# Second-pass masks moved to GpSimd fills, and a new order on four engines, in an attention and expert kernel

## The reference, cut to what matters

```python
xn = layernorm(x)                                   # x: (2, 1024, 256)
# causal attention, 16 heads of 16, with a linear position bias
scores = einsum(q, k) * 16**-0.5 + (pos_k - pos_q) * slope[h]
scores = where(pos_k > pos_q, -inf, scores)
attn = maximum(softmax(scores), 1e-10)
s = (attn @ v) @ out_w.T + out_b
# feed-forward: RMS norm, router over 32 experts, top 4, at most 128 rows each
y[e] = (silu(rows[e] @ w_gate[e]) * (rows[e] @ w_up[e])) @ w_down[e]
g = silu(xn + sum_of_chosen(w * y) + sigmoid(x @ w_sg) * shared_ffn(x))
out = x + s * g
```

## Time and profile before

| | |
|---|---|
| time, median of 3 runs | 646.54 us (644.6 to 648.15) |
| profiled execution, its own time | 642.44 us |
| span of the profiled execution | 640.8 us |
| TensorE busy | 562.8 us, 88% |
| VectorE busy | 475.2 us, 74% |
| ScalarE busy | 452.6 us, 71% |
| GpSimd busy | 269.1 us, 42% |
| mean granted clock of TensorE | 0.957 of 2.4 GHz |

### The profile page before, as it was taken

The page is one execution under the profiler, slowest core; times in us unless marked ns, Lnnn a source line. Parts: engine busy times, 40 slices in busy tenths (PEclk is TensorE's granted clock), DMA queues, the critical chain, the costliest instruction groups (busy, mean ns, idle before and its releaser), DMA issues.

```text
span 640.8 us, 17285 instructions
## 1 busy us (share of the span) xinstructions
PE 562.8 (88%) x4584; PEld 384.2 (60%) x4584; DVE 475.2 (74%) x1066; ACT 452.6 (71%) x1053; POOL 269.1 (42%) x632
## 2 busy tenths in 40 slices
PE   1699559688999899999999999999999999999992
PEld 1694227555666566666666666666666666666661
DVE  5997964657777867886787788777867886787465
ACT  2322564358877878887888788878888887888670
POOL 7630000215445355445544554455455345544403
PEclk9759869789999999999999999999999999999997
DMA  8991256552335334433444343434433436731147
GB/s 258 167 253 59 99 155 195 132 135 60 88 90 111 91 86 87 105 90 89 102 100 97 91 103 84 92 83 102 98 90 87 105 91 199 192 77 23 26 137 135
DMA packets 79537, 71.47 MB, mean 112 GB/s; under 512 B 18114, under 2 KB 70020, under 8 KB 79492
## 3 DMA queue, kind: packets, MB, share of 16 engines
q1 hardware_dynamic: 70292, 59.30, 34.1%
q0 software_dynamic: 9136, 11.80, 12.1%
q10 hardware_dynamic: 80, 0.03, 0.0%
HBM read 47.82 MB, written 23.59 MB: 111 GB/s over the span
## 4 chain that ended last, share of the span: by engine, by line
PE 49%; ACT 20%; issue 12%; DVE 10%; DMA 4%; SPq 3%; ACTq 1%; DVEq 0%; POOLq 0%; POOL 0%
ACT PSB L1062 10%; PE PSB L897 7%; PE PSB L791 6%; ACT PB L1071 6%; PE PSB L765 5%; PE PSB L813 5%; PE PSB L868 4%; PE PSB L810 4%; PE PSB L787 3%; PE PSB L889 3%; PE PSB L850 2%; PE PSB L666 2%; PE PSB L761 2%; DVE WDS L1281 2%; SPq L497 1%
## 5 line engine op out<-in xcount | busy, mean ns | idle before, releaser
L1346 DVE TENSOR_REDUCE NEGM<-PSB 128x1 f32<-128x1024 f32 (+7 forms) x256 | 192.2, 751 | 58.6 <-PE PSB L765 57.6
L1062 ACT ACTIVATE PSB<-PSB,NEGM 128x1024 f32<-128x1024 f32 (+7 forms) x256 | 183.5, 717 | 35.6 <-DVE NEGM L1346 35.4
L1071 ACT ACTIVATE PB<-PSB 128x128 f32<-128x128 f32 (+7 forms) x256 | 166.8, 653 | 35.5 <-PE PSB L791 33.6
L1352 DVE TENSOR_SCALAR PB<-PB 128x128 f32<-128x128 f32 (+7 forms) x256 | 114.2, 455 | 45.9 <-ACT PB L1071 44.4
L765 PE MATMUL PSB<-STACKS 111*128 111x512 bf16 (+3 forms) x384 | 105.8, 330 | 0.0
L791 PE MATMUL PSB<-STACKS 111*128 111x512 bf16 (+3 forms) x384 | 104.2, 326 | 0.0
L787 PE MATMUL PSB<-MK,IDB 128*128 128x128 bf16 x256 | 57.5, 225 | 22.7 <-ACT PSB L1062 16.4
L1656 POOL DMA_INDIRECT moe_rows<-YE,IDX x32 | 56.9, 1777 | 29.3 <-issue 29.3
L810 PE MATMUL PSB<-PB,VH 128*32 128x256 f32 x640 | 67.8, 384 | 0.0
L787 PEld LDWEIGHTS PSB<-MK,IDB 128*128 128x128 bf16 x256 | 24.5, 96 | 63.7 <-ACT PB L1071 39.2
L761 PE MATMUL PSB<-MQ,IDB 128*128 128x128 bf16 x256 | 58.2, 227 | 0.9 <-ACT UL L1049 0.5
(11 more groups left out here) (200 smaller groups left out, 1171.6 us busy)
## 6 DMA issues: line engine op xcount, KB each, us to landing
STACKS<-q_parts SPq DMA_DIRECT2D x192, 32.0 KB, 1.9
STACKS<-k_parts SPq DMA_DIRECT2D x192, 32.0 KB, 1.8
WGU<-in_L_ffn_w_gate_dram SPq DMA_DIRECT2D x32, 176.0 KB
WGU<-in_L_ffn_w_up_dram SPq DMA_DIRECT2D x32, 176.0 KB
WDS<-in_L_ffn_w_down_dram SPq DMA_DIRECT2D x32, 176.0 KB
q_parts<-PB SPq DMA_DIRECT2D x8, 384.0 KB, 2.6
XN<-in_L_attn_qkv_dram SPq DMA_DIRECT2D x4, 512.0 KB, 5.7
moe_rows<-XN SPq DMA_DIRECT2D x1, 2048.0 KB, 8.8
```

The source lines that it names most:

```text
L1062: act.activation(sc, sc, ACT.Exp, bias=NEGM[:, par, i:i + 1], accum_out=LSUM[:, par, i:i + 1]).then_inc(exp1_done, 1)
L1071: act.activation(PB[:, k % 2, prob_offset(s):prob_offset(s) + (s + 1) * P], psf[:, base:base + (s + 1) * P], ACT.Exp).then_inc(exp2_done, 1)
L1346: dve.tensor_reduce(NEGM[:, par, i:i + 1], psf[:, base:base + (i + 1) * P], AX_X, ALU.max, negate=True).then_inc(max_ready, 1)
L1352: dve.tensor_scalar(p, p, FLOOR, 0.0, ALU.subtract, ALU.max).then_inc(clamp_done, 1)
```

## The change

- `PB` gets another layout, in which the diagonal blocks of tiles 0 to 3, and those of tiles 4 to 6, are evenly spaced, so that one access pattern (`diagonal`) covers each group.
- In the second pass the mask product is left out for seven of the eight tiles; the score product starts the sum itself. In its place GpSimd fills the wrong half of the diagonal blocks in `PB` with 0 after the clamp (`fill_diagonal`): once for tiles 0 to 3 (512 columns, after the clamp of step 3), once for tiles 4 to 6 (384 columns, after the clamp of step 6). The first value batch waits for the second fill instead of the clamp.
- GpSimd's gather stands directly behind the scatter. The first fill comes behind the value copy, the second at the end of the phase.
- VectorE takes the 896-column maximum ahead of the clamp of the unit before (step 7) and of this unit's step 0. It also takes over the copy to `XET`, after its 768-column maximum.
- ScalarE does the weighing behind `exp_seed` and the 896-column exponential instead of ahead of them.
- After the last unit, early products 0 and 1 take the place of gates 4 and 5, and these gates come later.

```diff
@@ -83,9 +83,20 @@
 def prob_offset(s):
-    return s * (s + 1) // 2 * P
+    return 9 * P * s if s < NQ // 2 else P * (10 * (NQ - 1 - s) + 1)
+def diagonal(probs, tiles):
+    n = len(tiles)
+    if tiles.start < NQ // 2:
+        first, step, at = prob_offset(tiles.start), 9 * P, 0
+    else:
+        first, step, at = prob_offset(tiles[-1]) - 9 * P, 10 * P, 9 * P
+    return probs[:, first:first + step * n].rearrange("p (n c) -> p n c", c=step)[:, :, at:at + P]
+FILLED = (range(0, 4), range(4, 7))
 VALUE_BATCH = (range(0, 7), range(7, 8))
 LEAD = 2
 PROJECT_BANK = [2, 6, 7, 2, 6, 7, 2, 3]
@@ -299,6 +310,7 @@
         p2_ready = sem("p2_ready")
         exp2_done = sem("exp2_done")
         clamp_done = sem("clamp_done")
+        fill_done = sem("fill_done")
         pv_done = sem("pv_done")
         v_ready = sem("v_ready")
         o_evacuated = sem("o_evacuated")
@@ -784,12 +796,14 @@
                     pe.wait_ge(exp2_done, unit(it, k, NQ, s - 1))
                 w = P * (NQ - j)
                 key = KS[slot][0:ROWS, j * P:(j + 1) * P]
-                pe.matmul(psf[:, base:base + P], IDB[:, :], MK[:, :],
-                          start=True, stop=False, skip_group_check=True)
+                masked = s == NQ - 1
+                if masked:
+                    pe.matmul(psf[:, base:base + P], IDB[:, :], MK[:, :],
+                              start=True, stop=False, skip_group_check=True)
                 for c0 in reversed(range(0, w, 512)):
                     c1 = min(c0 + 512, w)
                     ins = pe.matmul(psf[:, base + c0:base + c1], key, QS[slot][0:ROWS, j * P + c0:j * P + c1],
-                                    start=(c0 > 0), stop=True, skip_group_check=True)
+                                    start=(c0 > 0 or not masked), stop=True, skip_group_check=True)
                 ins.then_inc(p2_ready, 1)
             def values(it, k, batch):
@@ -800,7 +814,10 @@
                     pe.wait_ge(o_evacuated, unit(it, k))
                     pe.wait_ge(v_ready, unit(it, k, 1, 1))
                     pe.wait_ge(c_turned, unit(it, k, 1, 2) if exists(it, k + 1) else UNITS)
-                pe.wait_ge(clamp_done, unit(it, k, NQ, VALUE_BATCH[batch][-1] + 1))
+                if batch == 0:
+                    pe.wait_ge(fill_done, unit(it, k, len(FILLED), len(FILLED)))
+                else:
+                    pe.wait_ge(clamp_done, unit(it, k, NQ, NQ))
                 for s, c in value_order(batch):
                     j, far = step_tile(s), NQ - 1 - c
                     probs = PB[:, par, prob_offset(s):prob_offset(s) + (s + 1) * P].rearrange("p (t q) -> p t q", q=P)
@@ -1135,10 +1152,6 @@
                 for s in range(NQ):
                     if s == 0 and exists(it, w - 1):
                         shared(it, w - 1, SB)
-                    if s == 2 and exists(it, w):
-                        o = aux_task(it, w, TR)
-                        act.activation(XET[:, :, :].rearrange("p c m -> p (c m)"), o[:, 0:D], ACT.Copy)\
-                            .then_inc(xet_ready, 1)
                     if s == 4 and exists(it, w):
                         shared(it, w, SA)
                     if s == 6 and exists(it, w):
@@ -1147,12 +1160,12 @@
                         exp2(it, k, s, exists(it, k + 2))
                     if s == 0 and isinstance(it, int) and k == UNITS - 2:
                         exp_seed(it, k + 1)
-                    if s == 1 and exists(it, w - 1):
-                        weigh(it, w - 1)
                     if s == 1 and exists(it, k + 1) and not (isinstance(it, int) and k == UNITS - 2):
                         exp_seed(it, k + 1)
                     if exists(it, k + 2):
                         exp1(it, k + 2, s)
+                    if s == 1 and exists(it, w - 1):
+                        weigh(it, w - 1)
                     if isinstance(it, int) and k == UNITS - 2 and s >= NQ - 3:
                         projected(s - (NQ - 3))
                     if isinstance(it, int) and k == UNITS - 1 and s == 0:
@@ -1351,6 +1364,12 @@
                 p = PB[:, k % 2, prob_offset(s):prob_offset(s) + (s + 1) * P]
                 dve.tensor_scalar(p, p, FLOOR, 0.0, ALU.subtract, ALU.max).then_inc(clamp_done, 1)
+            def turn_rows(it, k):
+                b, before = aux(it, k, TR)
+                dve.wait_ge(aux_ready[b], before + 1)
+                dve.tensor_copy(XET[:, :, :].rearrange("p c m -> p (c m)"), PSB[:, AUX + b, 0:D]).then_inc(xet_ready, 1)
             def turn_shift(it, k):
                 dve.wait_ge(c_flipped, unit(it, k, 1, 1))
@@ -1447,16 +1466,22 @@
                 w = k + LEAD
                 for s in range(NQ):
                     if isinstance(it, int) and k == UNITS and s == 1:
-                        for g in (4, 5):
-                            gate(g)
+                        for g in range(2):
+                            early_product(g)
+                    late = exists(it, k + 2) and exists(it, k - 1)
+                    if s == 1 and late:
+                        row_max(it, k + 2, s)
+                        clamp(it, k - 1, NQ - 1)
                     if s > 0 and exists(it, k):
                         clamp(it, k, s - 1)
-                    if exists(it, k + 2):
+                    if exists(it, k + 2) and not (s == 1 and late):
                         row_max(it, k + 2, s)
                     if s == 0 and exists(it, w - 1):
                         shared(it, w - 1, SB)
-                    if s == 0 and exists(it, k - 1):
+                    if s == 0 and exists(it, k - 1) and not late:
                         clamp(it, k - 1, NQ - 1)
+                    if s == 2 and exists(it, w):
+                        turn_rows(it, w)
                     if s == 3 and exists(it, k - 1):
                         evacuate_heads(it, k - 1)
                     if isinstance(it, int) and k == UNITS - 1 and s >= 3:
@@ -1476,10 +1501,10 @@
                         hidden_turned(it, w)
             phases(dve, phase)
-            for g in range(6, NT // 2):
+            for g in range(2, NT // 4):
+                early_product(g)
+            for g in range(NT // 4, NT // 2):
                 gate(g)
-            for g in range(NT // 4):
-                early_product(g)
             for g in range(NT // 4, NT // 2):
                 product(g)
                 add_input(g)
@@ -1542,6 +1567,14 @@
             pool.wait_ge(bias_ready, 1)
             pool.memset(VH[:, :, :, :], 0.0).then_inc(const_ready, 1)
             pool.wait_ge(xn_ready, NT)
+            def fill_diagonal(it, k, part):
+                tiles = FILLED[part]
+                hold(pool, clamp_done, unit(it, k, NQ, tiles[-1] + 1))
+                d = diagonal(PB[:, k % 2, :], tiles)
+                pool.affine_select(out=d, in_=d, compare_op=ALU.is_ge, fill=0.0, base=0,
+                                   pattern=[[0, len(tiles)], [1, P]], channel_multiplier=-1).then_inc(fill_done, 1)
             def chain(it, k):
@@ -1672,10 +1705,12 @@
                     chain(it, k + 1)
                 if exists(it, w - 1):
                     scatter(it, w - 1)
+                if exists(it, w + 1):
+                    gather(it, w + 1)
                 if exists(it, k + 1):
                     prepare_values(it, k + 1)
-                if exists(it, w + 1):
-                    gather(it, w + 1)
+                if exists(it, k):
+                    fill_diagonal(it, k, 0)
                 if exists(it, w) and w % SLOTS == 0:
                     copy_scales(it, w)
                     if w >= SLOTS:
@@ -1685,6 +1720,8 @@
                     b, before = aux(it, w - 1, SB)
                     hold(pool, aux_ready[b], before + 1)
                     copy_block(it, w + 1)
+                if exists(it, k):
+                    fill_diagonal(it, k, 1)
             phases(pool, phase, 1)
```

## The result

The changed kernel takes 662.16 us (median of 4 runs, 660.89 to 665.39), the kernel before 645.57 (4 runs, 643.0 to 648.15): ratio 1.0265, 95% interval 1.0206 to 1.0323, slower by 16.6 us. The profiled execution took 663.07 us with a span of 661.4, 20.6 us more than the span before.

What follows compares the result with a forecast made beforehand. The prediction took a new loop through GpSimd as the bound: 14.9 - 0.4 - 0.8 + 0.5 - 2.1 = +12.1 us, on the median of 646.54 a forecast of 658.5 us. Forecast's own range 651 to 668, wider range 643 to 674.

Steps and rivals of the forecast that it cites:

- a loop through GpSimd: First value batch through seed exponential and GpSimd's jobs to the second fill: 14.44 us in phases 2 and 1, 16.95, 16.36.
- a fill that starts in an open DMA row: Sign of being wrong: a GpSimd fill starting while a GpSimd DMA row is still open.
- the idle time before the batch: TensorE waits for the fill before the first value batch: about 2 us in phase 0, about 1 in phase 3.
- GpSimd's list in phase 2: GpSimd's jobs from the chain's first product: 9.71 us, plus 1.25 of fills and 0.25 lost beside clamps.
- moving the gather ahead of the value copy: GpSimd's job order: changes the order, not the sum; put at nothing (0 to 0.3 us more).
- order and masks as a gain of 0.35 us per unit: TensorE, ScalarE and VectorE loop: dropped masks and new order save 0.35 us a unit, in phase 3 0.42.
- The seven fours: Steady loop, units 1 to 28: 62.19 against 60.06 us for four units, +14.9 us in all.
- The phases outside them: Two full phases outside the fours save 0.2 us each, masks in the last two phases save 0.8.
- the new end order: End of the kernel: early products let two accumulating stores start sooner, between 0 and -2.8 us, taken as -2.1.
- Cheap fills: Rival: both fills take 0.57 us, nothing lost to clamps, four units 60.05, kernel 643.5 us; chance 0.20.
- GpSimd keeps up: Rival: GpSimd's DMA doesn't hold operations behind it, fill done before the batch, 633 us; chance 0.14.
- Dear fills or clamps: Rival: fills near 2.0 us or 0.8 us lost beside clamps, 18 us on top, 676.5 us; chance 0.14.

Runs made afterwards that it cites:

- e1: The changed kernel with the second fill directly behind the first, ahead of GpSimd's extra jobs: 650.61 us, ratio 1.014 to the kernel before.
- e3: The changed kernel with all masks kept, no fills, and the gather behind the value copy again: 653.97 us, ratio 1.0189 to the kernel before.
- e5: The changed kernel with all masks, no fills, gather behind the value copy, and the weighing ahead of the seed exponential: 634.05 us, ratio 0.9873 to the kernel before.
- e9: The changed kernel with masks, no fills, gather behind the value copy, and the weighing between seed and 896-column exponentials: 634.81 us, ratio 0.9888 to the kernel before.
- e6: The changed kernel with the second fill directly behind the first and the weighing between seed and 896-column exponentials: 648.35 us, ratio 1.0094 to the kernel before.
- e8: The changed kernel, but the last unit keeps its masks and has no fills: 659.83 us, ratio 1.0274 to the kernel before.
- e10: The changed kernel with fills moved into GpSimd's waits, weighing ahead of the seed exponential, last unit's masks kept: 644.55 us, ratio 1.0041 to the kernel before.

## Why the prediction was right, and where it was wrong

**Right: a loop through GpSimd, in phases 3 and 0.** Phase 3 came at 16.95 where 16.95 stood, phase 0 at 15.90 where 16.36 stood, and e1 took 0.8 us off each by moving one fill. The fills take 0.63 and 0.52 us and the pair 1.11, with the second fill right behind the first; I had 0.63, 0.51 and 1.25 with two gaps. The seed exponential starts 2.71 us after t0 (2.8 forecast), and ScalarE's 0.7 us wait at the weighing is gone, replaced by 0.54 before the 896-column exponential.

**Phase 0, 0.46 us too long.** Of this 0.10 lies before the chain. From the chain's first product to the end of the second fill it is 12.77 us (373.09 to 385.86), where I had 13.13. The DMA that adds the shared part now starts without the 0.26 us of issue time that rows 5 show ahead of it, and the second fill starts at 384.86, while that DMA's row is open to 385.30, and ends 0.56 after it. I had named a fill that starts in an open DMA row as a sign of being wrong, and this sign came. But the fill's row is 1.00 us long instead of 0.52, and it ends no earlier than a fill that starts behind the DMA would: by its end the DMA still held it back.

**Too large: the idle time before the batch.** I named some 2 us at phase 0 and 1 us at phase 3; the rows show 0.78 at the end of phase 0 and mostly 0.70 at the end of phase 3. The rest of the delay had moved ahead of it, into the shared product and, in phase 0, the shift rows.

**Right in sum, wrong in its terms: GpSimd's list in phase 2.** I took 9.71 us for the old jobs and 0.25 for clamps beside the chain. The jobs now take 10.23 (403.97 to the first fill at 414.20). The chain's second operation takes 0.70 us under the moved clamps, in the mean of 27 the row shows

```profile
L1597 POOL TENSOR_SCALAR CR<-CR 128x8 f32<-128x8 f32 x27 | 19.0, 703 | 5.3 <-POOL CR L1595 5.3
```

against 0.244 us in the kernel before. But the clamp that stretched the cast in rows 7 no longer falls on it (0.19 us instead of 0.48), so from its first product to the scatter the chain takes only 0.17 us more (5.55 against 5.38). The larger part, 0.35 us, comes from moving the gather ahead of the value copy: from the scatter's start to the end of these jobs it is 4.68 us, against 4.33 before. I had put this at nothing (0 to 0.3 more). The value copy itself is shorter (0.72 us, where beside a clamp it took 0.95), but it no longer runs in the gather's index wait. Shorter fills (0.14) and the earlier start (0.10) hide both, so 14.47 against 14.44 is in part luck.

**Wrong: order and masks as a gain of 0.35 us per unit.** This is the step that failed. I looked only at what waits on ScalarE when the weighing moves back (the exponential, which gains) and not at who waits for the weighing itself. That is the shared product, through the PSUM bank, on the engine that leads: 0.26 to 0.33 us of idle time in each unit of the changed kernel. Predicted were 14.25 and 14.4 us for phases 2 and 1 without fills; e3, which also keeps the masks, has 15.0 and 15.2, the changed kernel 14.8 and 14.95. So these two phases are set by this wait and the one for the shift rows, and not, as I wrote, by the loop through GpSimd, which is 14.47 long by the rows of phase 2. That their forecast was only 0.4 to 0.5 us off is luck. With the weighing ahead (e5) the rest of the order does gain: 59.25 against 60.0 for four, 0.2 us a unit. The idle time at ScalarE's fourth exponential, 0.71 to 0.78 us before, is still 0.57 to 0.64 there. And the masks gain as well: e3 to e1 is 62.0 to 60.95 with the gather moved too, 0.26 us a unit, 0.30 in phase 3 where I had 0.42.

Of the 2.7 us that four units of e3 lose to e5, four times 0.32 to 0.39 is the shared product, 1.3 us. The other 1.4 us lie in phases 0, 1 and 2, where the shift rows are waited for. (The waits view gives only 0.9 of a four to them, since it counts from the modelled end of the products before: in phase 0 it has 0.37 us, while this place comes 0.53 us later behind those products than in e5.) **Open:** why these rows land later. In phases 0 to 2 of e3 the gather starts 11.7 to 11.9 us after t0, just as they are under way, in e5 12.7 and later, in e9 12.3 and later, and neither e5 nor e9 waits for them. e6 has the weighing early too, but its gather of phase 0 starts at 11.7, and there the rows are waited for by 0.6 to 0.9 us. That the two transfers disturb each other fits all four, but it is argued, not shown: e9 was meant to test it and its gather came too late for that, and no run moved the gather alone.

**The sum, term by term** (spans, us). The seven fours were to add 14.9 and add 16.2. The phases outside them were to save 1.2: the last two save 0.3, but the first batch starts 3.8 us later. Of that 1.3 lie before the first widest maximum, which starts anywhere from 133 to 138 us in these kernels and says nothing, and 2.3 in the first two phases: 27.6 us against 25.3, with 27.2 in e3 and, with the weighing ahead, 25.0 in e5 (which of the waits makes them longer was not followed). The rest, from the batch of the unit before the last, was to save 1.6 and costs 0.9 (27.95 to 28.8): the last fill costs 3.1 (e8) instead of 0.5, and the new end order saves 2.25 (e5 and e8) or 1.35 (e3), where I had 2.1. Together 20.6 against 12.1. The medians miss by less (16.6 against 12.0), since the profiled execution lay 3.1 us below its median before and 0.9 above it after.

**The rivals.** Cheap fills needed fills of 0.57 us together and phase 0 at 15.4: they take 1.11 or more, and phase 0 takes 15.90. That no fill is waited for in phases 1 and 2, as it also had it, comes from another wait that makes them longer. GpSimd keeps up is refuted by e1 and by the 0.78 and 0.70 us. Dear fills or clamps: the fills in the loop cost what I took, and one operation of the chain pays 0.46 us, but the chain as a whole 0.17.

## What to carry to other kernels

When an operation is moved back on one engine, follow both its ends: what it frees on its own engine, and who waits for its result or for the buffer it reads. A PSUM bank that is handed on is such a dependency, and it is seen in no data flow. A small job added to a half-idle engine goes where that engine waits anyway (e10) and not at the end of its list. The sum of such an engine's jobs is no constant: GpSimd's list took 10.69, 11.34 and 11.87 us in phase 2 of three kernels, with the same jobs beside other VectorE operations. And before a transfer is made later, look for the one phase in which the queues are full: in e10 what the other phases gained was lost in two, by waits and by a lower clock behind them.

## What the runs showed of the hardware

A GpSimd fill over 384 columns took 0.52 us alone and 2.62 us beside one clamp and two VectorE operations with two inputs from SBUF (642.01 above). The other direction exists too. VectorE's clamps over 640, 768 and 896 columns in the changed kernel:

```profile
410.23 0.72 DVE L1365 TENSOR_SCALAR PB<-PB 128x640 f32<-128x640 f32 x1
411.77 0.54 DVE L1365 TENSOR_SCALAR PB<-PB 128x768 f32<-128x768 f32 x1
413.21 0.88 DVE L1365 TENSOR_SCALAR PB<-PB 128x896 f32<-128x896 f32 x1
```

and in the kernel before:

```profile
397.90 0.49 DVE L1352 TENSOR_SCALAR PB<-PB 128x640 f32<-128x640 f32 x1
399.50 0.54 DVE L1352 TENSOR_SCALAR PB<-PB 128x768 f32<-128x768 f32 x1
400.98 0.63 DVE L1352 TENSOR_SCALAR PB<-PB 128x896 f32<-128x896 f32 x1
```

The two that became longer lie beside the end of a GpSimd indirect DMA and a copy right behind it (410.67 to 411.39 and 413.50 to 414.23); the one between them lies beside neither. Which of the two operations stretches them, these rows don't separate. In the kernel before it is the other way round: the 768-column clamp keeps its 0.54 us beside GpSimd's value copy, and the copy takes 0.95 instead of 0.72. I had priced GpSimd's jobs as time on its own list alone.
